# Decoder layer on one core: the cross-attention mask is tested by GpSimd, the ones and queries of the passage are reordered, one square root moves to VectorE

## The reference

```python
x = x + attn(layernorm(x), w_qkv, w_proj, b_proj)   # 16 heads of 64; q, k, v, scores, softmax and outputs
                                                    # clipped and truncated to multiples of 1/4096
x = x + xattn(layernorm(x), ctx, ctx, mask, wo_w, wo_b)  # 16 heads of 8 over 1601 context rows; scores + mask
x = x + ffn(layernorm(x), ...)                      # 8 experts, the best 2 of each token, gated
def xattn(q, k, v, mask, wo_w, wo_b):
    scores  = einsum('bhqd,bhkd->bhqk', qh, kh) + mask      # mask: 4 x 1 x 256 x 1601
    ctx     = einsum('bhqk,bhkd->bhqd', softmax(scores), vh)
    return relu(ctx @ wo_w.T + wo_b)
```

## Time and profile before

| what | value |
|---|---|
| median of 3 runs | 679.93 us (675.46 to 682.39) |
| the profiled execution | 684.11 us, its span 682.4 us |
| busy share of the span | PE 81%, DVE 70%, ACT 69%, POOL 21% |
| chain that ended last | PE 42%, ACT 16%, DVE 16%, DMA 13%, SPq 4% |
| mean granted clock of PE | 0.924 of full speed |

### The profile page before, as it was taken

One profiled execution on the slowest core, in us unless ns is written; L12 is line 12 of the kernel. 1 busy time (PEld: TensorE's weight loads), 2 busy tenths in 40 slices (PEclk: granted clock), 3 DMA queues, 4 the chain that ended last, 5 costly groups with the idle time before them and its releaser, 6 DMA issues.

```text
span 682.4 us, 13903 instructions
## 1 busy us (share of the span) xinstructions
PE 552.4 (81%) x5115; PEld 304.1 (45%) x5115; DVE 477.6 (70%) x864; ACT 472.7 (69%) x850; POOL 140.2 (21%) x215
## 2 busy tenths in 40 slices
PE   5788887888773558999989998899896895799992
PEld 3455445544453423333333333333332242699991
DVE  3577867787860895888878888888885525566762
ACT  3889999999960208778768876778674865477760
POOL 5001001000030251350135010510003107233232
PEclk9999999999987759999999999999997877699995
DMA  8823727613859016210461019000005001111103
GB/s 234 246 96 109 189 106 180 208 65 119 243 166 192 3 59 210 77 49 3 104 164 33 19 24 216 31 1 2 2 1 188 2 1 49 40 39 42 45 28 100
DMA packets 31669, 62.89 MB, mean 92 GB/s; under 512 B 4526, under 2 KB 21338, under 8 KB 31156
## 3 DMA queue, kind: packets, MB, share of 16 engines
q0 software_dynamic: 8000, 40.91, 22.2%
q1 hardware_dynamic: 22020, 20.31, 10.1%
q10 hardware_dynamic: 1584, 0.79, 0.4%
HBM read 42.29 MB, written 19.30 MB: 90 GB/s over the span
## 4 chain that ended last, share of the span: by engine, by line
PE 42%; ACT 16%; DVE 16%; DMA 13%; issue 8%; SPq 4%; POOL 1%; POOLq 0%; ACTq 0%; DVEq 0%
DVE smax L1684 13%; PE pair L1098 11%; PE pair L1073 6%; PE pair L1262 6%; ACT region_p L1342 6%; PE pair L1028 5%; DMA region_k<-region_p 4%; PE pair L1250 3%; DMA kimg<-region_k 3%; ACT region_p L1350 3%; ACT region_p L1440 2%; ACT region_p L1334 2%; SPq L574 2%; PE pair L1272 1%; PE pair L928 1%
## 5 line engine op out<-in xcount | busy, mean ns | idle before, releaser
L1440 ACT ACTIVATE region_p<-pair 128x1024 f32<-128x1024 f32 (+3 forms) x277 | 217.5, 811 | 66.7 <-PE pair L1073 61.3
L1684 DVE TENSOR_REDUCE smax<-pair 128x2 f32<-128x1024 f32 x192 | 225.5, 1219 | 53.4 <-PE pair L1028 52.7
L1559 DVE SCALAR_TENSOR_TENSOR region_p<-region_p 128x1024 int16<-128x1024 int16 (+1 forms) x56 | 67.2, 1221 | 16.5 <-ACT region_p L1334 8.5
L1098 PE MATMUL pair<-region_p 128*32 128x256 f32 (+1 forms) x832 | 69.8, 410 | 0.5 <-ACT region_p L1447 0.4
L1098 PE MATMUL pair<-region_p,region_b 128*32 128x256 f32 (+1 forms) x832 | 66.5, 391 | 0.4 <-ACT region_p L1447 0.4
L1073 PE MATMUL pair<-region_b,region_k 59*128 59x256 bf16 (+1 forms) x416 | 54.7, 273 | 8.4 <-ACT region_p L1440 3.9
L1028 PE MATMUL pair<-region_k,region_b 56*128 56x512 bf16 (+1 forms) x256 | 44.1, 362 | 16.0 <-DVE smax L1684 14.8
L928 PE MATMUL pair<-region_p 128*64 128x256 f32 x256 | 35.6, 399 | 22.3 <-ACT region_p L1350 17.9
L1342 ACT ACTIVATE region_p<-region_p 128x256 f32<-128x256 int16 x128 | 51.6, 419 | 0.0
L1262 PE MATMUL pair<-region_p 128*128 128x128 f32 x368 | 45.8, 279 | 0.0
L1262 PEld LDWEIGHTS pair<-region_p 128*128 128x128 f32 x368 | 43.8, 195 | 0.0
(11 more groups left out here) (243 smaller groups left out, 950.3 us busy)
## 6 DMA issues: line engine op xcount, KB each, us to landing
kimg<-region_k SPq DMA_DIRECT2D x56, 200.1 KB
region_k<-kimg POOLq DMA_DIRECT2D x8, 1400.9 KB, 17.6
region_b<-in_mask_Bx1xSxS_ff POOLq DMA_DIRECT2D x12, 800.5 KB, 7.2
region_p<-in_mask_Bx1xSxS_ff POOLq DMA_DIRECT2D x4, 800.5 KB, 13.0
region_k<-in_L_ffn_W POOLq DMA_DIRECT2D x3, 1024.0 KB, 9.6
xdisp<-region_x POOLq DMA_DIRECT2D x1, 2322.0 KB, 17.9
region_b<-in_ctx SPq DMA_DIRECT2D x3, 768.0 KB
xdisp<-region_x POOLq DMA_DIRECT2D x1, 2257.5 KB, 16.7
```

What stands on the lines that cost most here:

```text
L1098: last = pe.matmul(pair[3][32 * h:32 * h + 32, 512 + s % 2 * S:512 + (s % 2 + 1) * S], v_heads[b % 2][0:rows, t, c:c + 32], pT[0:rows, n / ...
L1440: act.activation(pT[0:rows, first // 3 % 2, k:k + size], home[0:rows, 0:size], ACT.Exp).then_inc(expt_made, 1)
L1559: return dve.scalar_tensor_tensor(out_, floor16, 0.0, floor16, ALU.is_lt, ALU.add)
L1684: last = dve.tensor_reduce(units[:, :, c // 3, c % 3], both, AX.X, ALU.max)
```

## The change

1. POOL tests the mask: for each tile a comparison with 0 (twice, so that a nonzero element becomes 1), then six additions that fold 1601 columns to 26, in place. `mask_hi` is 128 x 8 x 26. ACT's probes are gone. The loads of the tiles are ordered as before but wait for POOL's own folds; tiles 6 and 7 are tested behind `keys_load(0, a)`.
2. POOL waits for the ones ahead of `mask_load(0)` and `keys_load(1, a)`, not behind them, and clears the padding there.
3. PE projects tiles 2-3, then transposes batch 0's queries, then projects tiles 4-5 and 6-7. The queries of batches 1, 2 and 3 are transposed after pairs 9, 11 and 13.
4. The maximum over `mask_hi` on DVE and its transpose on PE stand behind `make_attn` and `attn_transposes` of the last batch.
5. `experts_load` waits until group 14's shift has landed.
6. The square root for the sixth of the seven layer norm calls (`n == 5`, 6 tiles) is made on DVE, by a bit trick and three Newton steps: 14 small instructions in place of a reciprocal, and no `std_of(5)` on ACT.

```diff
-QUERIES_AT = KT + TAIL_AT
+QUERIES_AT = (9, 11, 13)
...
+            def mask_probe(u, slot):
+
+                pool.wait_ge(probe_loaded[slot], 16 * (u + 1) if slot else 16)
+                tile, size = mask_sb[:, slot, :], S2
+                chain.step(pool.tensor_scalar(tile, tile, 0.0, 0.0, ALU.is_equal, ALU.is_equal))
+                while size > FOLDED:
+                    half = size // 2
+                    first, rest = tile[:, 0:size - half], tile[:, half:size]
+                    fold = pool.tensor_tensor(first if size - half > FOLDED else mask_hi[:, u, :], first, rest, ALU.add)
+                    size -= half
+                    if size > FOLDED:
+                        chain.step(fold)
+                fold.then_inc(probe_made, 1)
+
             for u in range(1, NT - 1):
-                pool.wait_ge(probe_made, 2 * u)
+                mask_probe(u - 1, 1)
+                pool.wait_ge(probe_made, u)
                 probe_load(u, 1)
...
-            pool.wait_ge(probe_made, 2 * NT)
+            mask_probe(NT - 2, 1)
+            mask_probe(NT - 1, 0)
+            pool.wait_ge(ones_loaded, 64)
+            pool.memset(qnat_0.rearrange("p t h (a r) -> p (t h) a r", a=2)[:, :, :, KROWS:64], 0.0).then_inc(qpads_made, 1)
+            pool.wait_ge(probe_made, NT)
             mask_load(0)
...
-            pool.wait_ge(ones_loaded, 64)
-            pool.memset(qnat_0.rearrange("p t h (a r) -> p (t h) a r", a=2)[:, :, :, KROWS:64], 0.0).then_inc(qpads_made, 1)
...
             def experts_load():
 
+                pool.wait_ge(shift_loaded, 32 * (GROUPS - 1))
                 last = event_of(2 * KT * HG * (B - 1) - 1)
...
             attn_values(HP - 1, B - 1)
-            project_out(1)
+            project_out(1, (2, 4))
...
             queries_T(0, pair[0])
-            project_out(2)
+            project_out(1, (4, 6))
+            project_out(2, OUT_TILES[2])
...
-                    if p == QUERIES_AT:
-                        for b in range(1, B):
-                            queries_T(b, pair[2 + (b + 1) % 2])
+                    if p in QUERIES_AT:
+                        b = QUERIES_AT.index(p) + 1
+                        queries_T(b, pair[2 + (b + 1) % 2])
...
-                        if hp >= 1:
-                            mask_probe(hp - 1, 1, b)
                         round_qkv(hp + 1, b)
...
-                    if last:
-                        mask_probe(*((HP - 1, 0) if b < 2 else (HP - 2, 1)), b % 2)
...
-                if e == X2_AT:
-                    std_of(5, FFN_TILES[0])
...
+            def norm_root(tiles):
+
+                cut_ = slice(*tiles)
+                root, half, square = rstd[:, cut_], std[:, cut_], meanvar[:, cut_, 1]
+                chain.step(dve.tensor_scalar(half, var_eps[:, cut_], -0.5, None, ALU.mult))
+                chain.step(dve.tensor_scalar(root.bitcast(I32), var_eps[:, cut_].bitcast(I32), 1, None, ALU.logical_shift_right))
+                chain.step(dve.tensor_copy(square, root.bitcast(I32)))
+                chain.step(dve.tensor_scalar(square, square, -1.0, ROOT_MAGIC, ALU.mult, ALU.add))
+                chain.step(dve.tensor_copy(root.bitcast(I32), square))
+                for _ in range(3):
+                    chain.step(dve.tensor_tensor(square, root, root, ALU.mult))
+                    chain.step(dve.tensor_tensor(square, square, half, ALU.mult))
+                    chain.step(dve.scalar_tensor_tensor(root, square, 1.5, root, ALU.add, ALU.mult))
```

More of the change, by code:

```diff
@@ L32 @@
 LN_EPS = 1e-5
+ROOT_MAGIC = float(0x5F3759DF)
 LOWEST = -3.0e38
@@ L54 @@
 BURST = 12
+FOLDED = 26
 GROUPS = B * HG
@@ L229, in decoder_layer @@
         nmT = sb("nmT", [24, 2, 128], BF16)
-        mask_hi = sb("mask_hi", [128, 2 * NT])
+        mask_hi = sb("mask_hi", [128, NT, FOLDED])
         mask_any = sb("mask_any", [128, 1])
@@ L967, in head_pair @@
                         ctx_subtract(half, 1)
+                    attn_transposes(hp, b)
                     if last and b == B - 1:
@@ L970, in head_pair, with project_out @@
                         pe.transpose(any_row, mask_any[:, :], ident[:, :]).then_inc(any_T, 1)
-                    attn_transposes(hp, b)
                     if last and b == 2:
-                        project_out(0)
-            def project_out(c):
-                first, end = OUT_TILES[c]
-                pe.wait_ge(o_made, B * (HP - 1) + end // 2)
-                for i, t in enumerate(range(first, end)):
+                        project_out(0, OUT_TILES[0])
+            def project_out(c, tiles):
+                pe.wait_ge(o_made, B * (HP - 1) + (tiles[1] + 1) // 2)
+                for t in range(*tiles):
+                    i = t - OUT_TILES[c][0]
                     for n in range(HP):
@@ L982, in project_out @@
                                          wpT[:, n, :], start=(n == 0), stop=(n == HP - 1))
-                last.then_inc(proj_mm, 1)
+                if tiles[1] == OUT_TILES[c][1]:
+                    last.then_inc(proj_mm, 1)
             for hp in range(HP):
@@ L1350, in attn_move @@
                 act.activation(attnT, pair[1][:, :].bitcast(I16)[:, 0:1024], ACT.Copy).then_inc(attnT_made, 1)
-            def mask_probe(u, slot, half):
-                act.wait_ge(probe_loaded[slot], 16 * (u + 1) if slot else 16)
-                keys = slice(0, S2 // 2) if half == 0 else slice(S2 // 2, S2)
-                act.activation(mask_sb[:, slot, keys], mask_sb[:, slot, keys], ACT.Abs,
-                               accum_out=mask_hi[:, 2 * u + half:2 * u + half + 1]).then_inc(probe_made, 1)
             std_of(1)
@@ L1544, in layer_norm @@
                 cut_ = slice(*tiles)
-                dve.tensor_scalar(var_eps[:, cut_], meanvar[:, cut_, 1], LN_EPS, None, ALU.add).then_inc(var_made, 1)
-                if meanwhile:
-                    meanwhile()
-                dve.wait_ge(std_made, n)
-                chain.step(dve.reciprocal(rstd[:, cut_], std[:, cut_]))
+                last = dve.tensor_scalar(var_eps[:, cut_], meanvar[:, cut_, 1], LN_EPS, None, ALU.add)
+                if n == 5:
+                    chain.step(last)
+                    norm_root(tiles)
+                else:
+                    last.then_inc(var_made, 1)
+                    if meanwhile:
+                        meanwhile()
+                    dve.wait_ge(std_made, n if n < 5 else n - 1)
+                    chain.step(dve.reciprocal(rstd[:, cut_], std[:, cut_]))
                 for t in range(*tiles):
@@ L1613, in head_pair @@
                         make_dots(*batch_of(hp, b, 1))
+                    make_attn(hp, b)
                     if last and b == B - 1:
-                        dve.wait_ge(probe_made, 2 * NT)
-                        dve.tensor_reduce(mask_any[:, :], mask_hi[:, :], AX.X, ALU.max,
+                        dve.wait_ge(probe_made, NT)
+                        dve.tensor_reduce(mask_any[:, :], mask_hi[:, :, :], AX.XY, ALU.max,
                                           apply_absolute_value=True).then_inc(any_made, 1)
-                    make_attn(hp, b)
                     if b == 1 and not last:
```

2 lines of the change are left out of this document (1 added, 1 removed).

## The result

| | before | after |
|---|---|---|
| median | 677.69 us (675.02 to 682.39) | 711.83 us (709.54 to 715.4) |
| span of the profiled execution | 682.4 us | 713.6 us |
| mean granted clock of PE | 0.924 | 0.896 |

The ratio is 1.050, 95% interval 1.042 to 1.059, from four executions of each. In some executions a kernel runs 1.5% and more above its fastest; ratios, and where one such lies among them medians and ranges, leave these out. The change makes the kernel 5% slower; forecast were 654 us and 0.05 for any slowing of over 1%.

The account below looks back on a forecast made before the run. Bound: ACT nearly full in self-attention, then the ones' loads, DVE in the first sweep, later PE's waits and low clock. 10.8 + 1.8 + 8.8 + 4.6 = 26.0 us off 684.1 gives 658.1, median 654; range 637 to 672.

Parts of the forecast that it names:

- The probes come to POOL: Self-attention: POOL's mask test holds DVE 4.3 us a tile, 1.75 let through, 14 us lost; bounds 0 and 34.
- The slower rival: Self-attention: two-operation comparison holds DVE some 8 us a tile, 48 us through, 687 us; holds of 34 us and more 0.14.
- some 13 us better: Self-attention: how much better the forecast sum would be if DVE and POOL did not exclude each other in SBUF.
- the first rival: Self-attention: POOL's holds on DVE cost nothing; first reduction at 214, 10.7 us more gained, 643 us; chance 0.16.
- The probes leave ACT: Self-attention: removing ACT's mask probes gains 10.3 us, bounds 7 and 13.9.
- The passage: Self-attention's end to first reduction: ones land early, masks decide, first reduction at 224.7 instead of 235.5, 10.8 us gained.
- second reckoning: From DVE's readiness to first reduction by PE's projection: 14.6 us, first reduction at 223.9, just ahead of the masks' route.
- Queries among chunks: First sweep: three blocks of transposes cost 2.3 us in place of 4.11, 1.8 us gained; bounds 0 and 3.5.
- The expert loads behind the shift: Late cross-attention: group 14's shift back to 1.8 us gains 5.2, PE's clock staying up 3.6, together 8.8 us.
- The square root: Sixth layer norm: ACT's 3.2 us stretch goes, 1.0 charged for DVE, 2.4 from the clock; net 4.6 us, bounds 2 and 6.
- the signs named ahead: Trace signs of being right, such as POOL 72 us busier, truncations of 3 to 5 us, ones within 6 us of the image.
- the signs of being wrong: Truncations staying at 1.2 us, a comparison of 8 us, ones over 15 us, or a first reduction after 232.

Follow-up runs that it names:

- five versions: The kernel after, and the same with POOL doing comparison alone, comparison in pieces, additions alone or only clearings: 711.83, 687.4, 675.63, 670.98, 668.94 us.
- the bench's: Kernel before plus POOL and DVE instructions started together behind its last addition; beside the comparison a four-column TENSOR_SCALAR lasts 5.58 us, 0.17 alone.

## Why the prediction was wrong

**The failing step is "The probes come to POOL".** It counted 4.3 us of hold a tile on DVE and let 1.75 of it through. Measured: DVE is 56.1 us busier than with no test, 7.0 a tile, and the norm comes 62.2 later, 7.8 a tile. Three things in the step were off, and the third is the largest: with the measured 7.0 and the share of 0.41 that was let through, the loss would have been 23 us (an estimate from these numbers), with the measured share it is 62.
- *Which instructions are held.* It took the two-input ones alone, from one pair of additions. The one-input TENSOR_SCALAR of `make_attn` (+22.7 us) and of `esum4k` (+12.6, from 167 to 561 ns) are more than half of the 58.5 us by which DVE is busier than before; truncations have +11.0, the short ones of `make_o` +10.6. Beside the eight comparisons the one held longest was a full truncation three times (4.25 to 5.17 us), a short one of `make_o` three times (2.76 to 4.63) and a TENSOR_SCALAR twice (4.98 and 5.45): 3.9 us a tile in all, against 2.9. The rest, 3.1 a tile against 1.4, lies mostly on `make_attn` beside the additions. The section of the Trainium skill that the prediction cited names `tensor_scalar` as well. The trace of the kernel before gave little sign of it, since POOL does almost nothing in self-attention.
- *How long.* The comparison takes 5.64 us alone, not the clamp's 4.26, and 5.81 in the kernel; the first five additions take 4.5 us where 3.9 were counted.
- *What comes through.* "DVE's idle 4.85 us a pair" was set against the holds as if it could absorb them. But a hold of 4 to 6 us is one piece, and DVE's idle time lies in many. The chain ACT, DVE (`make_attn`), PE, ACT has no slack of that size: PE waited 48.2 us in 17 pieces for L1618, and five versions lost 0.8 to 1.1 us for each us of hold. The lower clock in self-attention (0.83 in the first 100 us against 0.98) goes with it; what it costs by itself is open.

**The slower rival came nearest; an end slower by over 1% had 0.05.** It said 48 us through; measured are 62.2. Its threshold, 5.1 us a tile, was passed by far. Its mechanism (a comparison of two operations holds DVE some 8 us a tile) is right in kind only: the comparison takes 5.64 us, and the forms held were more than it counted. (The "some 13 us better" for engines free of each other does not fit the 10.7 of the first rival; no term rests on it.)

**The probes leave ACT** was priced 10.3 us; the norm moves by 11.6 between the version with ACT's test and none. Right.

**The passage** came out near the forecast, but not by the route that was called decisive: 15.4 us from DVE's readiness to the first reduction forecast, by the masks, 15.2 measured in the kernel after. There self-attention ended so late that the masks had long landed, and the other route decided (second reckoning: 14.6): DVE waits for the projection.

```profile
259.12 7.36 PE L1001 MATMUL pair<-wpT,region_g 128*128 128x128 f32 x64
...
262.94 0.69 DVE L1670 SCALAR_TENSOR_TENSOR region_p<-pair,bproj_fx 128x512 int16<-128x512 f32 x1 [2.98 <-PE pair L1001]
```

The new wait for the masks shows where self-attention is short: 3.9 us with the test on ACT, 3.6 forecast, and 16.6 us from readiness to the first reduction. The ones landed 7.9 us behind the image's end, not 5.5, and 9 in the kernel after; within the bounds of 1.8 and 24, and hidden.

**Queries among chunks** was put at 1.8 and is 1.2 on the mean, with bounds of 0 and 3.5. The stall of 4.11 us is gone; two of 0.81 and 0.29 stand for it. But the block had lain beside group 0's shift, issued at 255.41 in the kernel before, which the second sweep waits for anyway. DVE's next stall, 3.66 us before, is 6.94 after, and that shift is now in the chain that ended last. The first line is of the kernel before, the second of the kernel after, the third of its chain.

```profile
267.78 3.49 DVE L1684 TENSOR_REDUCE smax<-pair 128x2 f32<-128x1024 f32 x3 [3.66 <-PE pair L1028]
...
304.15 2.36 DVE L1713 TENSOR_REDUCE smax<-pair 128x2 f32<-128x1024 f32 x2 [6.94 <-PE pair L1050]
...
293.47 7.13 DMA region_b<-nmT
```

**The expert loads behind the shift**: 8.8 forecast, 8.5 measured. In the chain that ended last, group 14's shift:

```profile
560.72 1.78 DMA wpT<-nmT
```

It was 7.03, and the windows of the 12 us behind have the clock at 1.00 in place of 0.58.

**The square root**: 4.6 forecast, 3.4 in the kernel after from the statistics to the first dispatch, of which up to 0.7 belongs to the repaired shift; over the versions 1.0 to 3.4, and nothing measurable by itself. PE's transposes now wait for DVE, which was charged 1.0 and is 1.57:

```profile
581.84 0.84 PE L875 MATMUL pair<-ident,region_x 128*128 128x128 f32 x6 [1.57 <-DVE region_x L1583]
```

Nor did the clock stay up altogether: it is 0.83 from 582 to 592 us, better than 0.62 but not 1.00.

**A loss that no step had**: 4.3 us between the splits of groups 9 and 10, by a fall of PE's clock (0.50 from 470 to 478 us, where it was 1.00 before). Between groups 5 and 6 it fell too (0.84 from 391 to 402 us, 1.00 before), for 1.6. The sum: forecast -26.0, measured +31.2, so 57.2 apart: self-attention 47.0, queries' stage 3.0, falls of the clock 6.2, the rest 1.0.

Of the signs named ahead: POOL's busy time (+87.5 for +72), truncations of up to 5 us (beside three comparisons of eight), head pairs with a tile above 22 us (27.2 to 35.8), no table load and a clock of 1.00 behind group 14 came. The two head pairs without a tile took 20.3 and 22.4 us, so one was not under 21. The ones landed 9 us behind the image, not within 6, and DVE's wait for the masks did not come. The signs that came fitted the slower rival as well. What would have told them apart, the length of `make_attn` and PE's wait for it, was not named; of the signs of being wrong, a first reduction after 232 came (271.5).

## What to carry to other kernels

Before work goes to an idle GpSimd, list every VectorE instruction beside it that reads two SBUF inputs or is a TENSOR_SCALAR within SBUF, and count a long GpSimd instruction (1.4 to 5.6 us here) whole as a hold on the first of them. Idle time of VectorE in small pieces doesn't absorb it: count all of the hold as lost, unless a trace shows slack in pieces of that length. In this kernel a TENSOR_REDUCE on VectorE or an activation on ScalarE cost less, and on GpSimd short instructions hurt less than long ones. Transfers that a stage waits for should be issued ahead of large ones that nobody waits for yet: here the ones alone brought the first reduction 10.6 us forward.

## What the runs showed of the hardware

On POOL a TENSOR_SCALAR of 1601 columns takes 5.64 us with two comparisons and 4.26 with one clamp (no run separates the number of operations from their kind); an addition of 801 columns 1.87, a clearing of 1601 columns 1.43.

A hold lasts as long as POOL's instruction beside 1601 columns or additions of 801 (1.94 us for a TENSOR_SCALAR of 0.35). Beside comparisons of 400 columns (1.56 us each) it was 0.2 to 0.35 us and more than one DVE instruction came through:

```profile
818.24 1.56 POOL L922 TENSOR_SCALAR region_k<-region_k 128x400 f32<-128x400 f32 x1
818.31 0.59 DVE L2250 TENSOR_SCALAR region_k<-region_k,rnorm 128x256 int16<-128x256 f32 x1 [1.52 <-POOL region_k L921]
818.83 0.34 DVE L2251 TENSOR_SCALAR region_k<-region_k,rnorm 128x256 int16<-128x256 f32 x1
```

This is less than a hold of the whole instruction, and no run explains it.

PE's clock fell at group 9's shift in some versions and not in others. Before the change PE waited 1.81 us there and its next groups of eight matmuls kept 0.64 us; after it waited 2.50 us, and the granted clock went from 1.00 to 0.50 at about 470 us:

```profile
468.43 0.40 PE L1095 MATMUL pair<-region_p,region_k 59*128 59x256 bf16 x4 [2.50 <-DMA region_p<-nmT]
468.76 0.64 PE L1120 MATMUL pair<-region_p,region_b 128*32 128x256 f32 x8
...
469.87 1.02 PE L1120 MATMUL pair<-region_p,region_b 65*32 65x256 f32 x8
...
471.38 1.08 PE L1120 MATMUL pair<-region_p,region_b 128*32 128x256 f32 x8
```

In sixteen traces this DMA took 3.6 to 4.1 us in ten, and the stage had the fall in all of them (24.3 to 26.8 us from group 9's to group 10's split). It took 2.8 to 3.5 us in six: five had no fall (20.9 to 21.6 us), one, the bench's, had it all the same (3.2 us and a wait of 1.88; 23.9 us). So the longer wait went with the fall each time, and the shorter one is no safe sign. Why the transfer is the longer in those ten was not tried. A version may thus gain or lose 4 us at a place that it does not touch.
